# Where a 100 KB tensor begins in on-chip memory: a transformer layer with top-1 experts, BIG moved from 64 past a multiple of 128 bytes to a multiple of 128

## What is computed

```python
x = x + xcond(ctx, layernorm(x), cond, cond, ln1, ln2, Wq, Wkv, Wo)   # 16 heads, softmax over 256 keys
y = layernorm(x)
e = argmax(y @ router);  g = sigmoid(score of e)
shared = silu(y @ ws1) * (y @ ws3) @ ws2                     # 256 -> 704 -> 256
routed = silu(g*y @ w1[e]) * (g*y @ w3[e]) @ w2[e]           # 256 -> 704 -> 256
out = x + shared + routed
```

## Time and profile before

| | us |
|---|---|
| median of 3 runs | 689.62 |
| lowest and highest run | 689.21, 689.84 |
| span of the profiled execution | 686.9 |
| PE busy in that span | 676.2 |
| DVE, ACT, POOL busy | 476.6, 431.1, 271.4 |

### The profile page before, as it was taken

How to read it: one execution, slowest core, us unless ns; L and a number is a source line. 1 busy time by engine, 2 the same in 40 slices (tenths; PEclk the granted TensorE clock), 3 DMA queues, 4 the chain that set the end, 5 groups by cost and what they waited for, 6 DMA issues and landing times. The chain is left out here.

```text
span 686.9 us, 18022 instructions
## 1 busy us (share of the span) xinstructions
PE 676.2 (98%) x5935; PEld 627.4 (91%) x5936; DVE 476.6 (69%) x985; ACT 431.1 (63%) x1166; POOL 271.4 (40%) x428
## 2 busy tenths in 40 slices
PE   8899999999999999999999999999999999999997
PEld 8789899899899998998998988898899999999997
DVE  7877887877877877887888676366636676444443
ACT  4987887878878888788788784332424553222222
POOL 2844243243243342433566641047420444433333
PEclk9999999999999999999999999999999999999999
DMA  7645545454455454455455433002676999787870
GB/s 277 188 125 139 134 135 147 121 147 140 123 149 142 114 150 137 124 146 142 129 138 163 124 93 122 8 1 93 174 243 196 305 360 288 258 261 261 260 240 8
DMA packets 77930, 111.69 MB, mean 163 GB/s; under 512 B 28732, under 2 KB 45758, under 8 KB 77632
## 3 DMA queue, kind: packets, MB, share of 16 engines
q1 hardware_dynamic: 66016, 92.73, 45.0%
q0 software_dynamic: 8864, 18.38, 9.3%
q10 hardware_dynamic: 3008, 0.03, 0.3%
HBM read 63.74 MB, written 16.67 MB: 117 GB/s over the span
## 5 line engine op out<-in xcount | busy, mean ns | idle before, releaser
L965 PE MATMUL PS<-BIG 128*128 128x256 f32 (+1 forms) x1164 | 196.0, 322 | 2.3 <-DVE BIG L777 1.9
L965 PEld LDWEIGHTS PS<-BIG 128*128 128x128 f32 x1164 | 166.1, 190 | 16.6 <-issue 3.0
L622 ACT ACTIVATE PR<-PS,NMX 128x256 f32<-128x256 f32 x256 | 118.1, 476 | 1.9 <-DVE NMX L790 1.9
L2011 PE MATMUL PS<-XST,W 128*128 128x128 f32 x1012 | 116.7, 275 | 0.0
L2011 PEld LDWEIGHTS PS<-XST,W 128*128 128x128 f32 x1012 | 115.0, 192 | 0.1
L631 ACT ACTIVATE PR<-PR,RINV 128x256 f32<-128x256 f32 x256 | 106.0, 518 | 0.0
L471 POOL DMA_DIRECT2D PT<-PR x128 | 65.0, 513 | 46.4 <-DVE PR L802 38.9
L802 DVE STREAM_TRANSPOSE PR<-PR 128x512 f32<-128x512 f32 x124 | 80.7, 685 | 2.8 <-ACT PR L631 1.9
L790 DVE TENSOR_REDUCE NMX<-PS 128x4 f32<-128x1024 f32 x64 | 75.5, 1198 | 0.0
L986 PE MATMUL PS<-KVF,WQ 128*128 128x128 f32 x512 | 65.6, 281 | 0.0
L1506 POOL DMA_INDIRECT out_x<-YS,WHO x23 | 32.2, 1400 | 84.0 <-DVE YS L1873 82.3
(11 more groups left out here) (186 smaller groups left out, 1124.6 us busy)
## 6 DMA issues: line engine op xcount, KB each, us to landing
PT<-PR SPq DMA_DIRECT2D x368, 64.0 KB, 2.3
W<-in_w SPq DMA_DIRECT2D x29, 640.0 KB
W<-in_w SPq DMA_DIRECT2D x21, 768.0 KB
PT<-PR POOLq DMA_DIRECT2D x128, 64.0 KB, 2.5
turned<-CXN SPq DMA_DIRECT2D x15, 256.0 KB, 2.0
INT<-turned POOLq DMA_DIRECT2D x56, 64.0 KB, 2.7
xs_sorted<-C SPq DMA_DIRECT2D x26, 128.5 KB, 3.1
W<-in_w SPq DMA_DIRECT2D x8, 352.0 KB
```

The costliest lines, as they stand in the source:

```text
L622: last = act.activation(probs, logits, ACT.Exp, bias=NMX[:, g, own, p % 2:p % 2 + 1], accum_out=SUM[:, p, own:own + 1])
L965: last = pe.matmul(dst, stat(s, k), mov(m, k), start=n == 0, stop=n == len(todo) - 1)
L2011: last = pe.matmul(h[:, P * c:P * (c + 1)], lhs13(W13[par], k, c), XST[par][:, :, k, :], start=k == 0, stop=k == KD - 1)
```

## The change

The call that allocates BIG moves ahead of the one for C. No instruction is added, removed or moved: on each of the five engines the program has the same instructions in the same order as before, and only addresses in their operands differ.

```diff
         mem = {
+            "BIG": sb("BIG", [128, BIG_SIZE], FP32R),
             "C": sb("C", [128, NB, DI]),
             "IDENT": sb("IDENT", [128, 128]),
...
-            "BIG": sb("BIG", [128, BIG_SIZE], FP32R),
             "RT": sb("RT", [128, KD, NE]),
             "RTS": sb("RTS", [128, KD, 2, NE], FP32R),
```

## The result

| | before | after |
|---|---|---|
| median of 8 runs, us | 689.64 | 690.90 |
| lowest and highest, us | 688.49, 689.91 | 690.00, 692.47 |
| span of the profiled execution, us | 686.9 | 689.1 |

The ratio is 1.0021, with a 95% interval from 1.0011 to 1.0030. By the medians the change costs 1.3 us, by the ratio 1.4 (0.8 to 2.1). That is small, but clear of no change, and the forecast was no change (689.5, range 687.0 to 693.0).

What follows compares the result with a forecast made beforehand. PE's pace through its own instructions was taken to bound the kernel. 686.9 + 0 + 0 + 0.08 = 687.0 us, plus 2.7 from span to median, gave 689.7, shaded to 689.5; range 687.0 to 693.0.

Steps and rivals of the forecast that it cites:

- part 1 of the sum: Matmuls with both operands in BIG: distance stays 0, cost 0; bounds 7.0 us less, 2.8 us more if unsettled.
- the first reading: PE's stationary load and moving stream disturb each other; address distance modulo 128 counts: 0 gives 120 ns, 64 gives 113.
- The two streams no longer fall into step: Rival: 512-column matmuls never settle with both rests at 0, up to 2.8 us more, 692.4 us; chance 0.18.
- the likeliest case by itself: Whole kernel: distance alone counts or nothing does, no change within the measurement; 688.0 to 690.6 us, chance 0.62.
- term 2: 391 matmuls of L2038, MRH/MRL over BIG, distance 32 to 96: 0 taken, ends -1.7 and +0.9 us.
- Term 3: Last output projection: 12 matmuls go from distance 64 to 0, +0.08 us.
- Parts 4 and 5: Other engines' accesses, and C, IDENT, transfers from C and the scoring matmuls: cost 0 each.
- the second: On PE's matmuls, an operand's own rest counts and a rest of 64 is bad; 7.0 us less if so.
- The own-rest rival: 256-column matmuls in BIG go to 113.3 ns as rest 64 becomes 0; -7.0 us, 682.6 us, chance 0.09.
- the falling floor: Rival: without straddled multiples of 128, loads alone set the pace of BIG's matmuls; 10.9 us saved, 678.7 us, chance 0.03.

Runs made afterwards that it cites:

- proj_only: Kernel before with BIG left in place and only WOH, WOL, OTH and OTL moved by 64 bytes modulo 256; ratio 1.0023.
- rest_back: Changed kernel with 192 unused bytes ahead of WOH, so that WOH, WOL, OTH and OTL stand to BIG as before; ratio 1.0001 against the kernel before.
- low_64: Changed kernel's order (BIG first) with unused bytes giving BIG rest 64 and all others their rest of before; ratio 1.0012 against the kernel before.
- shift_all: Kernel before with BIG at a multiple of 128 and every tensor behind it moved by the same 64 bytes; ratio 1.0005.
- gap_inside: Kernel before with 64 unused bytes inside BIG ahead of MID, tensors behind BIG moved by 128 bytes; ratio 1.0015.
- all_64: mid_64 with 32 more bytes each ahead of MRH and OTH; ratio 0.9976 against the kernel before, median 687.40 us.
- mid_64: Kernel before with 64 unused bytes ahead of MID and 192 behind it, KV unmoved modulo 256; ratio 0.9982.
- ot_only: Kernel before with only OTH and OTL moved by 64 bytes; ratio 1.0010.
- wo_only: Kernel before with only WOH and WOL moved by 64 bytes modulo 256; ratio 1.0002.

## Why the prediction was wrong

**The step that failed** is part 1 of the sum, "Both operands in BIG ... the distance stays 0. Cost 0 by the first reading." The distance inside the v_unit does stay 0, and its settled pace does stay 227 ns. But the cost was read from the settled pace alone, and only from the two operands of one matmul. A pair of v_units has 12 matmuls, and they are not settled from the first. How long the unsettled part is depends on the phase in which the output projection leaves them. The projection has no operand in BIG, so the sum had no term for it, yet its tensors moved relative to BIG (OTH from 224 to 32, WOH from 192 to 0). What the runs showed in place of the 0: 48 ns a pair, +1.39 us in the loop, whole with BIG unmoved (proj_only) and gone with BIG at a multiple of 128 (rest_back).

The sign was in the rows: the earlier trace rows had a stretch at 231 ns beside one at 227, and I used that only for the upper bound. The pair it lies in, the last one of the kernel before, goes 233 236 224 231 236 228 233 230 227 from its third distance on, which within 1 ns is how the loop's pairs go after the change.

The rival "The two streams no longer fall into step", at 0.18, named what would be seen, but not why. Its reason was both rests at 0; rest_back has that and loses nothing, proj_only has both at 64 and loses all. It was also about all 648 matmuls of 512 columns and never settling; in fact 348 of them settle later, and L1930 stays at 60.5 us. So its sign was right and its cause wrong. The stated range holds the measured 690.9 only because it made room for this rival; the likeliest case by itself, 688.0 to 690.6, doesn't hold it. The shading of the forecast to 689.5 went the wrong way, since term 2 went up and not down.

**Term 2** (MRH over BIG, 32 to 96): 0 taken, ends -1.7 and +0.9. Measured from the starts of all 391, +0.2 us. Right within its bounds. Its modulus was wrong: rests modulo 128 don't suffice (low_64).

**Term 3**: right, 113 to 120 ns over 12 matmuls, about 0.1 us. But distance 64 is not bound to 113: the same projection at the same distance goes at 113 ns in before and at 118 in shift_all and rest_back.

**Parts 4 and 5**: right. ACT's write of 512 columns to BIG still takes 598 ns and DVE's subtraction 682. The scoring matmuls start 112 ns apart both before and after.

With the three terms the sum becomes 1.4 + 0.2 + 0.1 = 1.7 us; the interval of the ratio says 0.8 to 2.1. One slip in the text changes nothing: at 113 ns L965's 256-column group would be busy for 99.8 - 5.1 = 94.7 us, not "near 94".

**The first reading against the second** (distance, not an operand's own rest) was right as far as it went, for the reason given: the pair (32, 0) and (96, 64) has the same pace. shift_all and rest_back show it for BIG at a multiple of 128. It was incomplete, since a distance of 64 has two paces, and the distance from one unit to the next counts too. The own-rest rival (682.6) and the falling floor (678.7) are out: no settled k_unit went below 118 ns in any run.

The Trainium skill's sentence that loading the next weights doesn't steal bandwidth from the running matmul (TensorE: Matmul & The Clock Gate, Step-by-step: what each phase is for) would have given 1.000 for every run here. The runs measured 0.9976 to 1.0030 from addresses alone.

## What to carry to other kernels

When a change moves only addresses, compare distances between the two operands of each matmul, and also between neighbouring units, since one unit hands its phase to the next. A pace read from the settled middle of a long run says nothing about the start of a run of 12. A multiple of 128 by itself brought nothing here; unused bytes that put stationary and moving operands of long runs 64 bytes apart brought 0.2%, and each such gap has to be read from the trace, stretch by stretch, as it can settle at either of two paces.

## What the runs showed of the hardware

- The same pair of shapes (128 stationary columns, 256 moving, fp32r, granted clock 1.0) settles at 113, 118 or 120 ns from start to start, and the distance of the two addresses modulo 256 decides in part. Distance 0 gave 120 for the k_units of every run that had it. Distance 64 gave 113 or 118: in gap_inside and all_64 two stretches of shared_out went at 113 and three at 118, in mid_64 one and four; L2038 in all_64 stayed at 118. The last output projection, at distance 64 in all of them, went at 113 in before and at 118 in shift_all, rest_back and ot_only. So the distance doesn't fix the pace; that the way a stretch is entered picks it is likely, but was not shown.
- 512 moving columns settle at 227 ns at distance 0, and alternate between 231 and 236 at distance 64 in gap_inside, the one run that has it. There the distance that is best for 256 columns is worse for 512.
- A unit's start repeats to 1 ns: 29 pairs in one execution at 2.827 us, and another kernel's at 2.875.
- PE's longest waits in the first units of the attention part differ between kernels whose v_unit pairs take equally long (before, shift_all, rest_back, wo_only): L965 for DVE 1.5 to 1.9 us, L1058 for ACT 0.4 to 1.1. Each kernel was profiled once, so whether the execution or the addresses make this difference is open. One span against another is therefore worth less than the length of one loop part.
- That a load and a moving stream disturb each other is the reading behind all this, and it was only argued: the runs show that the pace goes with the addresses, and nothing here looks inside the memory.
